# Graph attention kernel: the output norm's gamma and beta as two fused VectorE operations for each graph

## The reference

```python
# layer 0 (per graph)
nx = _ln(x, ln1_g, ln1_b)
q, k, v = nx @ wq + bq, nx @ wk + bk, nx @ wv + bv            # 8 heads of 32
bias = where(adj > 0, 0.1 * adj * adjf, -inf)
x1 = x + softmax(q k^T / sqrt(32) + bias) v @ wo + bo
x2 = x1 + gelu(_ln(x1, ln2_g, ln2_b) @ w1 + b1) @ w2 + b2
# layer 1 (per graph)
w = softmax(where(adj == 0, -inf, (x2 Wq)(x2 Wk)^T / 16))
y = x2 + (w @ (x2 Wv)) @ Wo + bo
mu = mean(y, -1); var = mean(square(y - mu), -1)
out = (y - mu) * rsqrt(var + 1e-5) * gamma + beta
```

## Time and profile before

| quantity | value |
|---|---|
| median of three runs | 981.6 us |
| the profiled execution | 982.47 us |
| its span (first to last instruction) | 980.7 us |
| PE busy | 921.9 us (94%), 7469 matmuls |
| DVE busy | 685.1 us (70%), 2573 instructions |
| ACT busy | 630.5 us (64%) |
| POOL busy | 389.5 us (40%), 261 instructions |
| granted TensorE clock | 0.986 of full on the mean |

### The profile page before, as it was taken

How to read it: one execution, slowest core, us unless ns; L and a number is a source line. 1 busy time by engine, 2 the same in 40 slices (tenths; PEclk the granted TensorE clock), 3 DMA queues, 4 the chain that set the end, 5 groups by cost and what they waited for, 6 DMA issues and landing times.

```text
span 980.7 us, 22213 instructions
## 1 busy us (share of the span) xinstructions
PE 921.9 (94%) x7469; PEld 812.9 (83%) x7469; DVE 685.1 (70%) x2573; ACT 630.5 (64%) x1857; POOL 389.5 (40%) x261
## 2 busy tenths in 40 slices
PE   7679999999999999999999999999999999998975
PEld 7567798888889888888988888898888889897864
DVE  4757776859587685958768595867859596777443
ACT  3376866748486675847677584867658385766452
POOL 2243343542435354342535434253544425333223
PEclk9799999999999999999999999999999999999988
DMA  8010000010100000000100000000000000000000
GB/s 258 1 33 12 23 23 23 23 33 0 32 21 32 21 25 29 0 32 21 32 21 32 21 18 15 20 32 21 32 21 21 25 7 27 11 23 1 23 1 32
DMA packets 29998, 26.53 MB, mean 27 GB/s; under 512 B 1142, under 2 KB 29708, under 8 KB 29964
## 3 DMA queue, kind: packets, MB, share of 16 engines
q1 hardware_dynamic: 29920, 26.09, 8.5%
q10 hardware_dynamic: 44, 0.01, 0.0%
HBM read 17.71 MB, written 8.39 MB: 27 GB/s over the span
## 4 chain that ended last, share of the span: by engine, by line
PE 80%; DVE 10%; issue 4%; ACT 4%; DMA 0%; DVEq 0%; ACTq 0%; POOL 0%
PE bank L291 18%; PE bank L293 17%; PE bank L292 17%; PE bank L436 6%; PE bank L417 5%; PE bank L409 3%; PE bank L503 3%; PE bank L529 3%; ACT bank L696 3%; DVE nx L914 2%; DVE stats L897 2%; PE bank L428 2%; PE bank L448 2%; PE bank L485 2%; PE bank L368 1%
## 5 line engine op out<-in xcount | busy, mean ns | idle before, releaser
L696 ACT ACTIVATE bank<-p_s,neg_max 128x128 f32<-128x128 f32 x512 | 182.5, 356 | 3.6 <-DVE neg_max L937 3.6
L1202 POOL TENSOR_TENSOR rstd<-ve,minus_half 128x4 f32<-128x4 f32 (+1 forms) x51 | 51.8, 1016 | 309.7 <-DVE ve L907 309.7
L291 PE MATMUL bank<-w_hi,hT_hi 128*128 128x256 f32 x512 | 147.1, 287 | 0.3 <-DVE hT_lo L840 0.2
L293 PE MATMUL bank<-w_hi,hT_lo 128*128 128x256 f32 x512 | 144.2, 282 | 0.0
L292 PE MATMUL bank<-w_lo,hT_hi 128*128 128x256 f32 x512 | 144.0, 281 | 0.0
L937 DVE CUSTOM_DVE_ANT_0 p_s<-bank,bias 128x128 f32<-128x128 f32 x512 | 112.6, 289 | 11.4 <-PE bank L409 11.4
L291 PE MATMUL bank<-n2T_hi,w_hi 128*128 128x512 f32 (+1 forms) x272 | 113.0, 415 | 4.7 <-ACT v L645 2.6
L712 ACT ACTIVATE bank<-bank,vec_cols 128x512 f32<-128x512 f32 (+1 forms) x136 | 86.5, 636 | 43.6 <-PE bank L293 40.4
L293 PE MATMUL bank<-n2T_hi,w_lo 128*128 128x512 f32 (+1 forms) x272 | 103.8, 382 | 0.0
L292 PE MATMUL bank<-n2T_lo,w_hi 128*128 128x512 f32 (+1 forms) x272 | 103.6, 381 | 0.0
L291 PEld LDWEIGHTS bank<-w_hi,hT_hi 128*128 128x128 f32 x512 | 96.4, 188 | 2.6 <-DVE hT_lo L840 0.7
(11 more groups left out here) (161 smaller groups left out, 2385.2 us busy)
## 6 DMA issues: line engine op xcount, KB each, us to landing
xs<-in_x SPq DMA_DIRECT2D x15, 512.0 KB, 3.8
out<-y SPq DMA_DIRECT2D x15, 512.0 KB, 2.9
adj_i<-in_adj SPq DMA_DIRECT2D x15, 256.0 KB, 2.8
xs<-in_x SPq DMA_DIRECT2D x2, 256.0 KB, 2.7
x2T_f<-in_L_gnn_w SPq DMA_DIRECT2D x1, 512.0 KB, 7.0
tT<-in_L_gnn_w SPq DMA_DIRECT2D x1, 512.0 KB, 8.9
y<-in_L_gnn_w SPq DMA_DIRECT2D x1, 512.0 KB, 9.1
vo<-in_L_gnn_w SPq DMA_DIRECT2D x1, 512.0 KB, 9.6
```

The costliest lines, as they stand in the source:

```text
L291: mm(out, a_hi, b_hi, start=first, stop=False)
L293: return mm(out, a_lo, b_hi, start=False, stop=last)
L696: last = run(bank[r][:, NODES * place:NODES * place + NODES], p_s[:, r, place, :], ACT.Exp, scale=-1.0, bias=neg_max[:, r, place:place + 1 ...
L1202: P.tensor_tensor(lns[n]["rstd"][:, 0:k], lns[n]["ve"][:, 0:k], minus_half[:, 0:k], ALU.pow).then_inc(ln_pool[n], 1)
```

## The change

The norm's last three steps become two fused operations on VectorE for each graph: `gained3` computes (y - mean) * gamma straight after the moments, without the inverse deviation, and `shifted3` computes y * rstd + beta in the place where norm3 stood. GpSimd keeps rstd and loses `gain` and `offset`; the stores wait for VectorE, and group 16's `finish_last` goes.

```diff
             def store(g):
-                sp.wait_ge(pool_out, 2 * g + 2)
+                sp.wait_ge(dve_out, graph0(g) + size(g))
...
-            for b, finished, count in ((0, pool_out, 2 * GROUPS), (1, dve_out, 2)):
-                sp.wait_ge(finished, count)
+            for b in range(2):
+                sp.wait_ge(dve_out, GRAPHS - 1 + b)
                 sp.dma_start(out[GRAPHS - 2 + b], y[:, b, :]).then_inc(out_store, 16)
...
-            def norm3(g):
-                normed(3, g, y, y)
-
-            def finish_last():
...
+            def gained3(g):
+
+                dve.wait_ge(ln_dve[3], ln0(g) + 2 * size(g))
+                dve.sem_inc(stand_dve, 1)
+                for b in range(size(g)):
+                    V.scalar_tensor_tensor(out=y[:, b, :], in0=y[:, b, :], scalar=lns[3]["mv"][:, b, 0:1],
+                                           in1=rows["gamma"][:, :], op0=ALU.subtract, op1=ALU.mult).then_inc(ln_dve[3], 1)
+
+            def shifted3(g):
+                dve.wait_ge(ln_pool[3], g + 1)
+                dve.wait_ge(ln_dve[3], ln_end(g))
+                dve.sem_inc(stand_dve, 1)
+                for b in range(size(g)):
+                    V.scalar_tensor_tensor(out=y[:, b, :], in0=y[:, b, :], scalar=lns[3]["rstd"][:, b:b + 1],
+                                           in1=rows["beta"][:, :], op0=ALU.mult, op1=ALU.add).then_inc(dve_out, 1)
...
                 if C:
                     moments(3, gc)
+                    gained3(gc)
                 if B:
                     h_low(gb, 1)
...
                 if C:
-                    norm3(gc)
+                    shifted3(gc)
...
-            norm3(GROUPS - 1)
-            finish_last()
+            gained3(GROUPS - 1)
+            shifted3(GROUPS - 1)
...
-                if C:
-                    gain(gc, size(gc))
-                    offset(gc, size(gc))
...
-            gain(GROUPS - 1, 1)
-            offset(GROUPS - 1, 1)
```

More of the change, by code:

```diff
@@ L218, in build @@
         pool_xbo, pool_x1b, pool_x2b = sem("pool_xbo"), sem("pool_x1b"), sem("pool_x2b")
-        pool_out = sem("pool_out")
         row_loads = [(rows["bo"], bo), (rows["b2"], b2), (rows["bo1"], bo1), (rows["gamma"], gamma),
@@ L1266, in x2_plus_bo @@
                 P.tensor_tensor(x2[:, 0:k, :], x2[:, 0:k, :], row_of("bo1", k), ALU.add).then_inc(pool_x2b, 1)
[L1268 to L1274, removed]
             def turn(gp, ga, gb, gc):
```

## The result

The kernel got slower. The median is 1006.5 us (1006.1 to 1008.5, four runs) against 981.8 us for the kernel before (981.5 to 982.6, four runs): a ratio of 1.0255 with an interval of 1.0237 to 1.0272, or +24.8 us.

What follows compares the result with a forecast made beforehand. TensorE bounds the kernel, delayed by VectorE's full stretch around avT. 0.80 + 20.04 + 1.48 + 1.1 + 1.67 − 1.41 = +23.7 us on the 981.6 median gives 1005.3 us, eight-in-ten range 999 to 1014.

Steps and rivals of the forecast that it cites:

- The bound: Steady turn, moments of group c to h_low(7): VectorE runs without a gap; work ahead of avT delays TensorE one for one.
- gained3, 1.59 us: Between moments(3) and h_low(1): +1.59 us a turn, about 1.1 waiting for h_low(1), the rest at avT.
- shifted3, 0.31 of which 0.08 would show: In norm3's place behind avT: 0.31 us more against 0.23 of slack for h_low(7), so 0.08 us of stall.
- groups 1 to 13: Loop turns of groups 1 to 12 at 1.67 us each, 20.04, plus group 13's +1.48.
- group 13's cover: Group 13's turn: group 16's shorter stats leave 0.11 us of cover at avT, so the turn costs +1.48 us.
- Group 15's turn, 1.67: gained3 fills VectorE's 0.23 us wait for rstd; TensorE already waits for h_low(4) behind norm3: +1.67 us.
- Rival 4: The clock falls at TensorE's new stands each turn: some 2.6 us more a turn, about 1039 us; chance 0.02.
- Groups 0 and 14 and the end: Group 0 +0.80 us (half a gained3), group 14 +1.1 at mlp_up(5), end in group 16 −1.41 (earlier last store).
- GpSimd's relief, nothing: Two operations of 2.4 us per full group leave GpSimd, which is not in the chain: costed at nothing.
- Rival 1: GpSimd's rstd holds VectorE off the SBUF port at gained3 and shifted3: 3.0 us a turn, about 1022; chance 0.10.
- Rival 2: TensorE's 0.69 us idle elsewhere in a turn absorbs part: 0.98 us a turn, 996 us; chance 0.06.
- Rival 3: Behind norm1, removing GpSimd's gamma and beta speeds VectorE, so time stays at 982 us; chance 0.02.

Runs made afterwards that it cites:

- no_shifted: Changed kernel with shifted3 left out for groups 0 to 15 (no inverse deviation or beta there; stores wait for gained3): 1006.0 us, ratio 1.0239.
- gained_behind: Changed kernel with gained3 moved behind avT and h_low(3), directly ahead of shifted3: 1010.2 us, ratio 1.0288.
- both_late: Changed kernel with gained3 moved ahead of the second residual2 and shifted3 ahead of the second avT copy, where VectorE waits: 980.6 us, ratio 0.9989.
- no_gained: Changed kernel with gained3 left out for groups 0 to 15 (no mean removal or gamma there): 985.2 us, ratio 1.0035.
- moments_late: Changed kernel with gained3, shifted3 and also the moments of y moved late, GpSimd's rstd(3) behind the masks: 973.4 us, ratio 0.9906.
- norm3_moments_late: Kernel before the change, with moments of y and norm3 moved late, GpSimd's rstd, gamma and beta behind its masks: 975.0 us, ratio 0.9919.

## Why the prediction was right

Forecast 1005.3 us, range 999 to 1014, slower with a chance of 0.97; measured 1006.5. Step by step:

- **The bound.** VectorE's stretch from the moments to h_low(7) was read as full, although the engine is busy for 70% of the span. `no_shifted`, `gained_behind` and `both_late` show it three ways.
- **gained3, 1.59 us.** Its pitch was right to the hundredth; its price was 1.62 (L427 to L435, and `no_shifted`), 0.03 more because it starts that much later behind ve, split over the two waits as described, 1.11 and 0.84 where "about 1.1 and the rest" was said. (The operations of residual3, its model, take 473 to 485 ns over the whole trace and not 476 to 480; nothing hangs on it.)
- **shifted3, 0.31 of which 0.08 would show.** The mechanism was right, the term too small: mlp_down up to the transposes of nx grew from 5.80 to 5.98 us, 0.18, and `no_gained` gives 0.19. The wait itself is the one forecast: the stopped product starts 0.07 us late. The other 0.1 us is its second matmul, 0.22 us behind the first for 0.12; I had priced the wait alone. With it a turn grew by 1.78 for 1.67. Twelve times 0.11 is 1.3 of the 1.4 us by which groups 1 to 13 exceeded their term. The last 0.1 is group 13's cover, which the ledger misses because it reads avT: TensorE's out projection in that turn moved from 859.20 to 883.75, 0.12 less than avT, as forecast.
- **Group 15's turn, 1.67.** It was 2.64 in the profiled execution, and the path was another. I had the delay arrive at h_low(4); TensorE stood 1.48 us for h_low(1), then ran eighteen matmuls at the lower clock, 1.51 us longer than at full, and had no wait for h_low(4). At full clock it would have met one: h_low(4) ended at about 982.57 (its start and 0.42 us), and mlp_down began at 983.79. So by estimate some 1.2 us is the clock's and the turn would have cost about 1.5 without it. Rival 4 thus happened here once, and not in the steady turns (1.00 throughout). The other three executions have no trace, so whether they paid it is not known.
- **Groups 0 and 14 and the end.** +0.84 for 0.80. +1.10 for 1.1, but by luck in part: that counts from avT of the turn before, and from TensorE's out projection there it is +1.22 (24.55 to 25.77). −1.33 for −1.41: rstd took 0.93 us for the 0.71 of the earlier trace rows, beside the two operations of gained3, and ended at 1003.42, 1.05 us after the first of them began, where I had put it at about 1.03 us; the other 0.06 are two hand-overs, 0.13 us from ve to gained3 and 0.19 from rstd to shifted3, for 0.10 and 0.16.
- **GpSimd's relief, nothing.** Right: `moments_late` and `norm3_moments_late` have the same turn.
- **Rival 1 (rstd holds VectorE off)** is refuted: no fused operation took more than 486 ns. The first two operations of shifted3 (from 534.32 on, 0.40 us apart) began while the rstd of 533.86 was still running, and took no longer for it.
- **Rival 2 (TensorE makes part of it good)** is refuted: outside the two stands TensorE idled 58.53 − 55.90 − 1.11 − 0.84 = 0.68 us in the turn, against 0.69 before.
- **Rival 3 (VectorE gets faster without GpSimd's work)** is refuted by the time, and at the place that it named: h_low(7) takes 0.69 us with gamma and beta beside it (526.81) and 0.69 without (541.08). `norm3_moments_late`, which has that work elsewhere in the turn, has the turn of `moments_late`.

What the total doesn't settle: the profiled execution lies 2 us over the median. It paid for two falls of the clock, 0.8 us at the start and the one in group 15's turn; whether the other executions had them is not known. That forecast and median lie within 1.2 us is partly luck, since the falls and the longer low clock of the kernel before (−0.92) were in no term. The low-clock stretch between the last stages lasts differently from kernel to kernel: the mean was 0.68 over eight microseconds before; after, four microseconds at 0.57 are followed by full clock,

```profile
959.77:963.77 4.00, 3.80 (x10) 3.03 (x11) 0.15 (x1) 0.60 (x1) 0.72 (x2) 0.57 0.00 0
```

and in `both_late` the clock stays at 0.50 from 964 on to the end of the work; its profiled execution is one of its two slowest (983.1 us for a median of 980.6), which fits, though one trace doesn't show the cause. What sets the length is open; the stage cost 0.9 us less here, and so the turn is the cleaner measure of all kernels here.

## What to carry to other kernels

An engine that is idle for 30% of the span can still be the bound in a stretch of each turn; find the stretches in its timeline in which it has no gap, and count what is put into them at full price, and what fits into a gap elsewhere at nothing. The same eight operations cost 25 us in one place and none in another, and taking the moments (0.50 us of VectorE a turn) out of the full stretch was worth 6 to 7 us (980.6 to 973.4; 981.3 to 975.0 with the old norm). Some 6 of them are one place in the twelve turns of the loop, 0.51 us each, where the profile shows a wait of 0.40. A stand that is moved to a neighbouring place in the same full stretch is not removed.

## What the runs showed of the hardware

- Two engines side by side slowed each other in one direction only. rstd on GpSimd grew from 1.04 to 1.26 us beside gained3, and from 0.71 to 0.93 at the end; the VectorE operations kept 474 to 486 ns either way, also those that began behind a running rstd. The Trainium skill's page "SBUF — State Buffer", section "Who interferes with whom", says that the instruction that starts first holds the port for its whole length. The trace agrees for GpSimd as the one that is slowed, not for rstd as the holder.
- A stop in the middle of a stream costs TensorE some 0.1 us beyond the wait: in mlp_down the second matmul follows the stopped one after 0.22 us in place of 0.12, behind a stop of 0.07 us and behind one of 1.5 alike (542.04, and 482.87 in `gained_behind`). At the start of mlp_up(5) there is no such cost: the second matmul follows after 0.34 us with the stand of 1.11 us and without it.
- Stands of 1.11 and 0.84 us in a steady turn left the granted clock at 1.00. A stand of 1.48 us in group 15's turn was followed by 0.50, one of 1.47 in the same turn of `no_shifted` was not; the early one of 1.94 us was followed by 0.50 in two traces of eight. So a fall behind one stand in one trace is no proof that the stand caused it.
